# Sums over four steps, paired transposes in the product ring, field sums on VectorE, and gathers tied to products

## The reference

```
e = stack([tbl_0[ids[:, 0]], ..., tbl_31[ids[:, 31]]], axis=1)     # 2048 x 32 x 64
z = sum(e, axis=-1)                                                # 2048 x 32
outer = einsum('bpd,pde,bpe->bp', e[:, II], kernels, e[:, JJ])     # 2048 x 496 pairs i<j
h = concatenate([z, outer, dense_ctx], axis=1)                     # 2048 x 544
h = maximum(h @ W_top1 + b_top1, 0)                                # 512 columns
h = maximum(h @ W_top2 + b_top2, 0)                                # 256 columns
y = h @ W_top3
```

## Time and profile before

| what | value |
|---|---|
| median of 3 runs | 942.61 us (942.41 to 942.64) |
| the profiled execution's own time | 942.61 us |
| its span, first to last instruction | 940.8 us |
| granted TensorE clock, mean | 0.996 |
| PE busy | 889.5 us (95%) |
| DVE busy | 588.2 us (63%) |
| ACT busy | 139.7 us (15%) |
| POOL busy | 484.0 us (51%) |

### The profile page before, as it was taken

One profiled execution on the slowest core, in us unless ns is written; L12 is line 12 of the kernel. 1 busy time (PEld: TensorE's weight loads), 2 busy tenths in 40 slices (PEclk: granted clock), 3 DMA queues, 4 the chain that ended last, 5 costly groups with the idle time before them and its releaser, 6 DMA issues.

```text
span 940.8 us, 11425 instructions
## 1 busy us (share of the span) xinstructions
PE 889.5 (95%) x4592; PEld 280.6 (30%) x4592; DVE 588.2 (63%) x500; ACT 139.7 (15%) x209; POOL 484.0 (51%) x518
## 2 busy tenths in 40 slices
PE   0389999999999999999999999999999999999997
PEld 0122222332333323232333333323333333222232
DVE  0146777777655577767764477767775457777850
ACT  0020202012122020020020311002021212002001
POOL 6777777777777777777775346656630000000000
PEclk9989999999999999999999999999999999999999
DMA  9411111111211111121111001111100000000000
GB/s 334 148 26 27 28 27 27 27 27 27 47 28 27 27 27 27 27 47 27 27 27 21 15 14 23 24 38 23 23 16 1 1 0 1 1 2 20 1 1 0
DMA packets 21018, 29.60 MB, mean 31 GB/s; under 512 B 9188, under 2 KB 9316, under 8 KB 20840
## 3 DMA queue, kind: packets, MB, share of 16 engines
q0 software_dynamic: 16384, 16.81, 9.2%
q1 hardware_dynamic: 4576, 12.07, 3.5%
q10 hardware_dynamic: 8, 0.01, 0.0%
HBM read 27.79 MB, written 1.06 MB: 31 GB/s over the span
## 4 chain that ended last, share of the span: by engine, by line
PE 73%; POOL 19%; issue 6%; DMA 1%; ACT 0%; DVE 0%; DVEq 0%; ACTq 0%
PE y L505 39%; PE acc L519 20%; POOL rows L282 19%; PE y L548 6%; PE y L563 3%; PE spin L491 3%; PE spin L530 1%; PE y L553 1%; PE y L572 1%; DMA rows<-tbl,ids_sb 0%; DMA ids_sb<-ids 0%; ACT h L388 0%; DVE prod L462 0%; DVEq L198 0%; ACT h L400 0%
## 5 line engine op out<-in xcount | busy, mean ns | idle before, releaser
L462 DVE TENSOR_TENSOR prod<-y,xt 128x1024 f32<-128x1024 f32 x496 | 587.6, 1220 | 319.5 <-PE y L505 319.5
L282 POOL DMA_INDIRECT rows<-tbl,ids_sb x512 | 483.3, 944 | 210.4 <-issue 151.2
L505 PE MATMUL y<-xt,kw 64*128 64x512 f32 x1984 | 506.5, 624 | 4.7 <-ACT xt L337 4.7
L519 PE MATMUL acc<-prod,ones_strip 128*32 128x512 f32 x1984 | 265.9, 608 | 0.6 <-DVE prod L462 0.6
L505 PEld LDWEIGHTS y<-xt,kw 64*128 64x128 f32 x1984 | 170.1, 187 | 300.7 <-issue 294.0
L337 ACT COPY xt<-spin 128x512 f32<-128x512 f32 x64 | 37.5, 585 | 500.2 <-PE spin L491 500.2
L519 PEld LDWEIGHTS acc<-prod,ones_strip 128*32 128x32 f32 x1984 | 39.1, 108 | 190.2 <-issue 166.0
L491 PE MATMUL spin<-ident,rows 128*128 128x128 f32 x256 | 43.8, 296 | 40.4 <-DMA rows<-tbl,ids_sb 40.4
L548 PE MATMUL y<-h_in,w_sb 128*128 128x512 f32 x128 | 57.1, 599 | 0.7 <-ACT h_in L366 0.7
L491 PEld LDWEIGHTS spin<-ident,rows 128*128 128x128 f32 x256 | 28.0, 145 | 91.4 <-issue 63.9
L548 PEld LDWEIGHTS y<-h_in,w_sb 128*128 128x128 f32 x128 | 23.7, 190 | 34.2 <-issue 32.6
(11 more groups left out here) (19 smaller groups left out, 41.8 us busy)
## 6 DMA issues: line engine op xcount, KB each, us to landing
rows<-tbl,ids_sb POOLq DMA_INDIRECT x512, 2.4
kw<-pair_k SPq DMA_DIRECT2D x14, 512.0 KB, 11.4
w_sb<-w SPq DMA_DIRECT2D x1, 1024.0 KB, 12.8
sums<-z_sums SPq DMA_DIRECT2D x4, 256.0 KB, 2.5
w_sb<-w SPq DMA_DIRECT2D x1, 512.0 KB, 13.7
z_in<-sums SPq DMA_DIRECT2D x8, 64.0 KB
kw<-pair_k SPq DMA_DIRECT2D x1, 384.0 KB, 17.7
ids_sb<-ids SPq DMA_DIRECT2D x1, 256.0 KB, 2.8
```

The source lines that it names most:

```text
L282: pool.indirect_dma_start(out=rows[:, s, c, h, :], out_offset=None, in_=tables[f], in_offset=bass.IndirectOffsetOnAxis(ap=ids_sb[:, t, c * ...
L462: nc.vector.tensor_tensor(prod[:, n % PROD_SLOTS, :, :], y_banks[u % Y_SLOTS][:, :, :], x, ALU.mult).then_inc(y_read, 1)
L505: last = nc.tensor.matmul(y[:, h, :], kw[part, d, :], xt[part, slot_of(t, units[h][0] // 2), :], start=True, stop=True)
L519: last = nc.tensor.matmul(acc[32 * q:32 * q + 32, :], ones_strip[:, 30 - 2 * s:62 - 2 * s], prod[:, (N_STEPS * t + u // 2) % PROD_SLOTS, u ...
```

## The change

**Groups of four.** `GROUP` is 4: four steps follow each other, then 8 matmuls sum the group before. `PROD_SLOTS` grows from 4 to 8, and there are two `acc` banks in turn.

**Transposes in the y ring.** The bank `spin` is gone. A transposed couple takes a place in the ring of three y banks, as a step does. From couple (1, 0) on, two couples are transposed at once into the two halves of a bank, and one ACT copy of 128x1024 moves both. All places of a later tile are multiples of 4: the couples at 4, 16, 32, 48, 64, 80, 96 and 112, the layers at 8, 16, 24 and 32. In the first tile the pairs of tile 1 stand at 108, 112, 116 and 120.

**Field sums.** DVE sums the gathered rows of each couple over the 64 numbers (one reduction of 128x512 numbers for a couple, 64 in all) into `z_rows`, the dense numbers are loaded beside them, and PE transposes `z_rows` (4 small transposes for a tile, at step 56, in the first tile at 104) through the y ring to `z_in`. The way through memory is gone.

**Gathers.** Each of the 8 DMAs of a couple of tiles 1 to 3 waits until a given number of products has been made: the first DMA of a pair for the product 32 steps ahead of the pair's transpose, and each following one for one product more. A slot of `rows` also needs the couple's field sums before it is used again.

```
-GROUP = 2
+GROUP = 4
...
-    for j in range(AHEAD):
-        work[N_STEPS - 5 * (AHEAD - j)].append(("transpose", 1, j))
+    work[N_STEPS - GROUP * (AHEAD // 2 + 1)].append(("fields", 0, 0))
+    for j in range(0, AHEAD, 2):
+        work[N_STEPS - GROUP * (AHEAD - j) // 2].append(("couples", 1, j))
...
-            work[j * N_STEPS // COUPLES + 2].append(("transpose", *divmod(n, COUPLES)))
+            work[j * N_STEPS // COUPLES // GROUP * GROUP + GROUP].append(("couples", *divmod(n, COUPLES)))
...
+GATHER_LEAD = 32
+def steps_before_gather(t, k, i):
+    what = Y_ORDER[copy_use(t, k)]
+    count = 2 * rowsets(t)
+    return STEPS_BEFORE[what] - GATHER_LEAD + (i + count * (k - what[2])) * 2 * TILE // P // count
...
                     if n >= GATHER_SLOTS:
-                        pool.wait_ge(spin_full, spin_use("transpose", *divmod(n - GATHER_SLOTS, COUPLES)) + 1)
+                        pool.wait_ge(y_full, copy_use(*divmod(n - GATHER_SLOTS, COUPLES)) + 1)
+                        pool.wait_ge(fields_summed, n - GATHER_SLOTS + 1)
...
+                            if t > 0:
+                                pool.wait_ge(y_read, steps_before_gather(t, k, rowsets(t) * h + c))
...
-                nc.scalar.copy(xt[:, slot_of(t, k), :], spin[:]).then_inc(spin_read, 1)
+                nc.scalar.copy(xt[:, s:s + count, 0:w], y_banks[u % Y_SLOTS][:, 0:count, 0:w]).then_inc(act_read, 1)
...
+            def field_sums(t, k):
+                n = couple(t, k)
+                dve.wait_ge(gathered[n % GATHER_SLOTS], rows_in(n))
+                if k == 0 and t > 0:
+                    dve.wait_ge(y_full, y_use("fields", t - 1, 0) + 1)
+                nc.vector.reduce_sum(z_rows[:, 0:rowsets(t), 0, 2 * k:2 * k + 2],
+                                     rows[:, n % GATHER_SLOTS, 0:rowsets(t), :, :], axis=mybir.AxisListType.X
+                                     ).then_inc(fields_summed, 1)
...
+            def transpose_couples(t, k, count):
+                for h in range(count):
+                    n = couple(t, k + h)
+                    pe.wait_ge(gathered[s], rows_in(n))
+                    if h == 0:
+                        y = take_y(copy_use(t, k))
+                    for c in range(rowsets(t)):
+                        last = nc.tensor.transpose(y[:, h, P * c:P * c + P], ...)
+                last.then_inc(y_full, 1)
```

More of the change, by code:

```diff
@@ L61 @@
 PAIRS = FIELDS * (FIELDS - 1) // 2
-assert N_STEPS % GROUP == 0 and 4 * UNITS // 2 >= PAIRS and sum(K_CHUNKS) == N_STEPS
+assert sum(WIDTHS) == BATCH and N_STEPS % GROUP == 0 and 4 * UNITS // 2 >= PAIRS and sum(K_CHUNKS) == N_STEPS
 def step_at(*step):
@@ L124, in later_tile_work @@
     work = {d: [] for d in range(N_STEPS)}
-    for j in range(COUPLES):
+    for j in range(0, COUPLES, 2):
         n = COUPLES * t + AHEAD + j
         if n < COUPLES * TILES:
-            work[j * N_STEPS // COUPLES + 2].append(("transpose", *divmod(n, COUPLES)))
+            work[j * N_STEPS // COUPLES // GROUP * GROUP + GROUP].append(("couples", *divmod(n, COUPLES)))
     for d, what in zip(MLP_STEPS, (("mlp1", t - 1, 0), ("mlp1", t - 1, 1), ("mlp2", t - 1, 0), ("mlp3", t - 1, 0))):
-        work[d + GROUP].append(what)
+        work[d].append(what)
     work[6].append(("extra", t, 0))
@@ L133, in later_tile_work @@
         work[step_at("inner", s - 1, 2) + 10].append(("extra", t, s))
+    work[56].append(("fields", t, 0))
     return work
@@ L157, with copy_use, act_uses_through, copied @@
 PLAN = [what for t in range(TILES) for what in plan(t)]
[L159 to L169, removed]
+Y_ORDER = [what for what in PLAN if what[0] not in ("sum", "extra")]
+Y_USES = {what: u for u, what in enumerate(Y_ORDER)}
 def y_use(*what):
     return Y_USES[what]
-def mlp_uses_through(u):
-    return sum(what[0] != "step" for what in Y_ORDER[:u + 1])
+def copy_use(t, k):
+    for what in (("couple", t, k), ("couples", t, k), ("couples", t, k - 1)):
+        if what in Y_USES:
+            return Y_USES[what]
+def act_uses_through(u):
+    return sum(what[0] != "step" for what in Y_ORDER[:u + 1])
+def copied(t, k):
+    return act_uses_through(copy_use(t, k))
+GATHER_LEAD = 32
+STEPS_BEFORE = {}
+_steps = 0
+for _what in PLAN:
+    STEPS_BEFORE[_what] = _steps
+    _steps += _what[0] == "step"
+def steps_before_gather(t, k, i):
+    what = Y_ORDER[copy_use(t, k)]
+    count = 2 * rowsets(t)
+    return STEPS_BEFORE[what] - GATHER_LEAD + (i + count * (k - what[2])) * 2 * TILE // P // count
 def slot_of(t, k):
@@ L228, in tower_program @@
         y_banks = [bank(f"y{i}", [P, 2, TILE]) for i in range(Y_SLOTS)]
-        acc = bank("acc", [P, TILE])
-        spin = bank("spin", [P, TILE])
+        accs = [bank(f"acc{i}", [P, TILE]) for i in range(2)]
         ids_loaded = sem("ids_loaded")
@@ L256, in couple, with rows_in @@
             return COUPLES * t + k
-        def copied(t, k):
-            return spin_use("transpose", t, k) + 1
-        COUPLE_IN = ROWSETS * 2 * 16
+        def rows_in(n):
+            return sum(16 * 2 * rowsets(m // COUPLES) for m in range(n % GATHER_SLOTS, n + 1, GATHER_SLOTS))
         @block.gpsimd
@@ L458, in _ @@
                 if m0 == m1:
-                    x = xt[:, m0:m0 + 1, :].to_broadcast([P, 2, TILE])
+                    x = xt[:, m0:m0 + 1, 0:w].to_broadcast([P, 2, w])
                 elif m0 < m1:
-                    x = xt[:, m0:m1 + 1:m1 - m0, :]
-                nc.vector.tensor_tensor(prod[:, n % PROD_SLOTS, :, :], y_banks[u % Y_SLOTS][:, :, :], x, ALU.mult
+                    x = xt[:, m0:m1 + 1:m1 - m0, 0:w]
+                nc.vector.tensor_tensor(prod[:, n % PROD_SLOTS, :, 0:w], y_banks[u % Y_SLOTS][:, :, 0:w], x, ALU.mult
                                         ).then_inc(y_read, 1)
+            for what, t, n in PLAN:
+                if what == "couple":
+                    field_sums(t, n)
+                elif what == "couples":
+                    field_sums(t, n)
+                    field_sums(t, n + 1)
+                elif what == "step":
+                    multiply(t, n)
         @block.tensor
         def _(pe):
[L467 to L471, removed]
             def take_y(u):
@@ L552, in mlp1 @@
                     j = 2 * pair + h
-                    last = nc.tensor.matmul(y[:, h, :], w1z_sb[part, j * P:(j + 1) * P], z_in[part, :],
+                    last = nc.tensor.matmul(y[:, h, 0:w], w1z_sb[part, j * P:(j + 1) * P], z_in[part, 0:w],
                                             start=False, stop=True)
@@ L577, in _ @@
             for what, t, n in PLAN:
-                if what == "transpose":
-                    transpose_couple(t, n)
+                if what == "couple":
+                    transpose_couples(t, n, 1)
+                elif what == "couples":
+                    transpose_couples(t, n, 2)
                 elif what == "step":
```

212 lines of the change are left out of this document (106 added, 106 removed).

## The result

The changed kernel takes 912.67 us (median of 4 runs, 912.37 to 914.36), the kernel before 942.62 on the same chip: ratio 0.9686, 95% interval 0.9669 to 0.9703. Predicted was 912.8. The profiled execution is the 914.36 one, with a span of 912.6 us; the prediction had 911.0 of span. The other three executions have spans of 910.6 to 911.2 us. So the prediction hits the median and is 1.6 us short of the execution that the trace shows, and the parts have to be looked at one by one.

A forecast was written before the change was run, and what follows sets the result against it. PE bounds the kernel, behind POOL's gathers in tile 0. 940.8 - 31.1 - 7.4 - 8.5 + 13.9 + 3 + 0.3 = 911.0 us of span, plus 1.8: 912.8 us, forecast range 907 to 919.

The forecast's parts named there:

- What bounds: Whole kernel: PE busy 889.5 of 940.8 us; tile 0 ends when POOL has fetched 24 couples, then PE's speed counts.
- Groups of four, -31.1: PE, step (1, 4) to (3, 120): 0.34 us of switching saved per four steps, 91 times, groups of 5.49 us.
- Transposes, -7.4: PE between the same steps: 19 paired transposes at 1.02, at most 1.18 us, cost 19.4 us instead of 26.8.
- field sums, -8.5: PE loses three times 3.44 us of field sums and gains three times 0.59: 8.5 us less.
- DVE's reductions cost nothing: DVE, after paired transposes: 64 reductions taken at 0.6 us; up to 0.88 us each costs nothing.
- The gathers' waits: POOL, tile 0 into tile 1: 144th gather issues 9 us late (8 to 13), step (1, 4) 13.9 us later.
- The clock, +3: PE, start of tile 1: idling before gathers lowers the granted clock to 1.2 GHz; the third loss counts, 3 us.
- The end, +0.3: Last four steps and what follows: 38.8 us instead of 38.5, 0.3 us more.
- the gates did hold gathers back: Rival for tile 0, chance 0.15: gates hold nothing back, POOL keeps its pace, 904 us.
- the fourth step was not late: Rival in PE's groups, chance 0.15: fourth step waits for its bank, or DVE's reductions are long, 919 to 930 us.
- the switch did not grow: Rival on PE, chance 0.05: the switch grows with the run, so groups of four gain nothing, 944 us.
- gathers kept their 1.25 us: Rival on POOL, chance 0.04: waits lengthen gathers until they bound the kernel; at 0.5 us each, 984 us.

## Why the prediction was right, point by point

- **What bounds.** Right: PE from step (1, 4) on, POOL ahead of it. The experiment with groups of four in the kernel before shows it best, for tile 0 stayed as long as it was. The chain has short pieces of DVE and ACT too behind 906 us, which the reading left out; they belong to the end.
- **Groups of four, -31.1.** Right, shown twice: 5.49 us a group in the trace, and 30.5 us behind step (1, 4) when undone. The switch does not grow with the run, from two steps to four.
- **Transposes, -7.4, and field sums, -8.5.** The durations came as taken, 1.02 us a pair and 0.59 for the field sums' transposes. With them, (1, 4) to (3, 120) should take 641.24 - 47.0 = 594.2; it takes 873.81 - 277.03 = 596.8, of which 2.3 are the low clock. The whole adds up to 0.3 us. The experiment with groups of two shows the two terms together, 16.2 us against the 15.9 put; they were not undone one by one.
- **DVE's reductions cost nothing.** Right from step (1, 4) on: 676 ns each instead of 0.6, two in 1.27 us, 0.71 us to spare and no late step. VectorE: DVE Perf Modes in the Trainium skill (the perf-mode tier table) gives a reduction one element a cycle only, an estimate of 0.53 us at its clock; the trace has 676 ns for a reduction by itself and 0.6 in a row. The limit is near: the fourth step had 0.14 us of room, where 0.3 less the loading of weights was put.
- **The gathers' waits.** Right in kind, and the one term that was too small: +13.9 was put, +16.0 came, because the 144th gather was 11 us late and not 9. The step that failed is that groups of four bring product 76 forward by 5 us, to 169. It ended at 170.77, 3.3 us earlier than before; product 91 followed 22.5 us later instead of 22, and the 144th gather 0.27 us behind it. In tile 0 PE catches up with the gathers and waits for them, and then works at the low clock, as PE's timeline of the changed kernel shows at 76 us, with a window of it:

```profile
75.05 0.66 PE L536 MATMUL y<-ident,rows 128*128 128x128 f32 x4 [1.48 <-DMA rows<-tbl,ids_sb]
76.38 1.66 PE L551 MATMUL y<-xt,kw 64*128 64x512 f32 x4 [0.68 <-ACT xt L353]
77.97 3.03 PE L567 MATMUL acc<-prod,ones_strip 128*32 128x512 f32 x16
80.94 3.70 PE L551 MATMUL y<-xt,kw 64*128 64x512 f32 x16
...
76.40:78.00 1.60, 1.60 (x8) 0.31 (x9) 0.00 (x0) 0.00 (x0) 1.29 (x2) 0.64 0.17 27
```

  The sum here takes 80.94 - 77.97 = 2.97 instead of 1.85 us, the step 1.59 instead of 1.06: 1.7 us. Three more steps of tile 0, at 110, 122 and 151 us, wait 0.24 to 0.25 us for a product, because the couple ahead of them has taken a place in the y ring; the kernel before with groups of four, which has `spin`, does not wait there. Not every execution loses the 1.7 us. In the traces without gates and with moved places, whose PE program is the same up to there, PE keeps full speed at this point, and product 76 ends at 169.6, 4.5 us earlier than before. With product 91 at 192.1 there and 0.27 us more, the 144th gather would be 9.9 us late in such an execution, an estimate, and not 11.1. So part of the hit is luck: the sum came near the median of the runs, whose executions other than the traced one were 1.4 to 2.0 us shorter and have no trace. The idle stretches came at 4.1, 10.9 and 5.3 us instead of 5, 13.5 and 8, which moves nothing, since the gathers set the end of each.
- **The clock, +3.** It cost 2.3. By the rule of the Trainium skill's page TensorE: Matmul & The Clock Gate (its table on why this matters) idle gaps bring the clock down; the trace agrees, at 0.50 to 0.53 after each of the three waits.
- **The end, +0.3.** Right: 38.8.
- **Sum.** 940.8 - 31.1 - 7.4 - 8.5 + 16.0 + 2.3 + 0.3 = 912.4, measured 912.6.

The rivals fell: the gates did hold gathers back (11 us, shown by their removal), the fourth step was not late from step (1, 4) on, the switch did not grow, and gathers kept their 1.25 us.

## What to carry to other kernels

Count the switches between kinds of matmul, not only the matmuls: longer runs of a kind gave 28 us by one line here, while PE read 95% busy before. And when the consumer gets faster, look again at where its program asks for data that a slower producer hands out at a fixed pace: moving a few transposes and opening the waits gave as much once more. A wait that spaces out transfers is safe only while the counter it waits for runs ahead of the transfers' own pace.

## What the runs showed of the hardware beyond the expected

- On three other chips the kernel before took about 20% longer, 1117 to 1136 us against 942.6, with a mean granted clock of 0.92 to 0.94 against 0.99 to 1.00. It was not traced there; the changed kernels were, and show waits that the profile gives to no engine or queue of theirs. Whether the chip or something else causes it stays open.
- A wait on a gather that is met already costs no time that the profile shows: with moved places POOL issues its 145th to 208th gather every 1.248 us with the waits and 1.249 before without them. In the changed kernel a gather that has to wait starts 0.27 us after its product ends at the earliest, and the first of a couple, which waits for three things, 0.80.
- At 76 us of tile 0 the changed kernel met the low clock, 0.64 in the window, after PE had waited 1.48 us for a gather; the kernel without gates waited 0.49 us at this point and the kernel before not at all, and both kept full speed.
